# Storing each bf16 part once, reading rows twice, and five copied blocks in place of three

## What is computed

```python
q = (layernorm(x) @ Wq + bq).reshape(B, S, H, DK)      # B 8, S 512, H 16, DK 16
k = (ctx @ Wk + bk).reshape(B, S, H, DK)
v = (ctx @ Wv + bv).reshape(B, S, H, DK)
scores = einsum('bqhd,bkhd->hbqk', q, k) / sqrt(DK)
attn = softmax(scores.reshape(H * B, S, S), axis=0)    # over all heads and batches
x = x + tanh(g_xattn) * (einsum('hbqk,bkhd->bqhd', attn, v) @ Wo + bo)
x = x + tanh(g_ffn) * ffn(layernorm(x))                # int8-like fake quantisation
```

## Time and profile before

| What | Value |
|---|---|
| Median of three runs | 854.2 us (851.15 to 855.73) |
| Profiled execution | 855.71 us, span 853.6 us |
| TensorE, VectorE, ScalarE, GpSimd busy | 740.9, 757.1, 680.9, 474.8 us |
| `prepare` | 0 to 130.2 us, DMA share 0.85 |
| `maxima` | 130.2 to 315 us, DMA share 0.66 |
| `attend`, `ffn` | 315 to 853.6 us |
| Moved by DMA | 165.87 MB |
| Stores of the blocks | 80 of 256 KB |
| Copies in DRAM | 20, of 512 KB or 1,024 KB |

### The profile page before, as it was taken

How to read it: one execution, slowest core, us unless ns; L and a number is a source line. 1 busy time by engine, 2 the same in 40 slices (tenths; PEclk the granted TensorE clock), 3 DMA queues, 4 the chain that set the end, 5 groups by cost and what they waited for, 6 DMA issues and landing times. The chain is left out here.

```text
span 853.6 us, 20038 instructions
## 1 busy us (share of the span) xinstructions
PE 740.9 (87%) x8129; PEld 447.5 (52%) x8151; DVE 757.1 (89%) x825; ACT 680.9 (80%) x1094; POOL 474.8 (56%) x225
## 2 busy tenths in 40 slices
PE   8897897777777769999999999999999999559977
PEld 6564372111212225677666777677777677424334
DVE  4799646999999978999999999999999995758957
ACT  3444448999999979899998999999999834759873
POOL 1233454000000000999999999999999997415500
PEclk9999998999999989999999999999999999879989
DMA  9897798766766627668867787868867794000014
GB/s 294 276 305 225 218 276 208 197 174 172 194 175 174 239 91 235 186 185 281 264 190 206 236 291 212 225 197 288 260 194 213 242 312 138 0 1 1 1 50 147
DMA packets 98442, 165.87 MB, mean 194 GB/s; under 512 B 9712, under 2 KB 37104, under 8 KB 98032
## 3 DMA queue, kind: packets, MB, share of 16 engines
q1 hardware_dynamic: 98352, 164.60, 64.3%
HBM read 134.42 MB, written 42.73 MB: 208 GB/s over the span
## 5 line engine op out<-in xcount | busy, mean ns | idle before, releaser
L1011 POOL TENSOR_TENSOR e<-e,recip 128x1792 f32<-128x1792 f32 (+3 forms) x128 | 367.9, 2919 | 19.3 <-DVE recip L1042 19.2
L963 ACT ACTIVATE e<-psY 128x512 f32<-128x512 f32 x512 | 296.3, 646 | 33.7 <-PE psY L896 28.2
L1029 DVE TENSOR_REDUCE partial<-e 128x128 f32<-128x4096 f32 (+1 forms) x80 | 283.3, 3559 | 7.2 <-ACT e L963 7.2
L896 PE MATMUL psY<-arena 128*128 128x128 bf16 x2048 | 200.6, 221 | 1.8 <-DMA arena<-k_stack 1.7
L896 PEld LDWEIGHTS psY<-arena 128*128 128x128 bf16 x2048 | 149.3, 98 | 75.8 <-issue 26.1
L699 ACT ACTIVATE copies<-ps_max 128x1024 bf16<-128x1024 f32 x189 | 175.9, 1045 | 0.6 <-PE ps_max L678 0.6
L892 PE MATMUL psY<-shift,minus 128*128 128x512 bf16 x396 | 153.1, 387 | 10.9 <-PEq L633 5.5
L715 DVE TENSOR_TENSOR high<-copies,high 128x3072 bf16<-128x3072 bf16 x63 | 109.8, 1744 | 0.0
L1002 POOL MEMSET ones_w<- 96x128 bf16 x1 | 0.2, 206 | 174.0 <-POOLq L633 174.0
L912 PE MATMUL psX<-e,arena 128*32 128x128 f32 x2048 | 76.2, 288 | 3.0 <-issue 1.3
L296 POOL TENSOR_TENSOR parts<-rest,parts 128x512 bf16<-128x512 f32 x32 | 37.5, 1177 | 73.7 <-ACT parts L440 73.6
(11 more groups left out here) (170 smaller groups left out, 1005.8 us busy)
## 6 DMA issues: line engine op xcount, KB each, us to landing
arena<-k_stack SPq DMA_DIRECT2D x256, 256.0 KB, 3.3
arena<-q_stack SPq DMA_DIRECT2D x64, 256.0 KB, 4.4
k_stack<-parts SPq DMA_DIRECT2D x40, 256.0 KB, 3.6
q_stack<-parts SPq DMA_DIRECT2D x40, 256.0 KB, 3.5
arena<-in_x_dram SPq DMA_DIRECT2D x8, 1024.0 KB, 10.8
k_stack<-k_stack SPq DMA_DIRECT2D x12, 512.0 KB, 11.4
arena<-in_ctx_dram SPq DMA_DIRECT2D x4, 1024.0 KB, 6.7
arena<-q_stack SPq DMA_DIRECT2D x8, 512.0 KB, 8.2
```

What stands on the lines that cost most here:

```text
L896: last = nc.tensor.matmul(bank[:, j * P:(j + 1) * P], ks[:, i % KRING, b * P:(b + 1) * P], qs[:, h, b * P:(b + 1) * P], start=False, stop= ...
L963: nc.scalar.activation(e_at(p, half * HB, (half + 1) * HB).rearrange("p q z i -> p z q i"), ps[n % SCORES][:].rearrange("p (z q i) -> p z ...
L1011: nc.gpsimd.tensor_tensor(part, part, by_pairs(recip[:, r % 2, :], share), ALU.mult).then_inc(pool_scaled, 1)
L1029: nc.vector.tensor_reduce(partial[:, :, k, :], e[:, t:t + n].rearrange("p t q z i -> p q i t z"), AX.XY, ALU.add).then_inc(sum_done, 1)
```

## The change

Each part is written once: keys to blocks 0, 1, 2 and queries to blocks 0, 3, 6, three stores for each unit, 48 in all. The arrangement of the finished stacks is another one, with the same eight products: keys 0 1 2 0 1 2 0 1, queries 0 0 0 1 1 1 2 2. The other five blocks of each chunk are copied, in two transfers for the keys (three blocks, then two) and two for the queries (blocks 1, 4, 7, then 2, 5). That is 16 transfers of 1,536 or 1,024 KB, issued 2, 2, 3, 2, 3, 2, 2, 0 behind the loads of the eight couples. Since the maxima use only written blocks, `load_pair` reads key blocks 0 and 1 twice (two transfers of 32 partitions for a key tile) and each of query blocks 0 and 3 twice (four transfers of 16 partitions for a head). A couple has 12 load transfers in place of 4, with the same bytes, and the semaphore counts follow.

```diff
--- before.py
+++ after.py
@@ -37,13 +37,13 @@
 
 
 
-K_PARTS = (0, 0, 1, 1, 2, 2, 0, 1)
-Q_PARTS = (0, 1, 0, 1, 0, 1, 2, 2)
-K_WRITTEN = (0, 1, 2, 3, 4)
-Q_WRITTEN = (0, 1, 2, 3, 6)
+K_WRITTEN = (0, 1, 2)
+Q_WRITTEN = (0, 3, 6)
 WRITES = len(K_WRITTEN)
-K_COPIED = ((5, 4, 1), (6, 0, 1), (7, 2, 1))
-Q_COPIED = ((4, 0, 2), (7, 6, 1))
+K_COPIED = (((3, 6), (0, 3)), ((6, 8), (0, 2)))
+Q_COPIED = (((1, 8, 3), (0, 7, 3)), ((2, 6, 3), (0, 4, 3)))
+K_MAX_ROWS = ((0, 2), (0, 2))
+Q_MAX_ROWS = ((0, 1), (0, 1), (3, 1), (3, 1))
 
 
 def row_copies(is_q, c):
@@ -53,16 +53,16 @@
 
 STACK_COPIES = (row_copies(0, 0) + row_copies(1, 0) + row_copies(0, 1) + row_copies(0, 2) + row_copies(0, 3)
                 + row_copies(1, 1) + row_copies(1, 2) + row_copies(1, 3))
-COPIES_A_COUPLE = 3
+COPIES_OF_COUPLE = (2, 2, 3, 2, 3, 2, 2, 0)
 
 
 def copy_rows(sp, k_stack, q_stack, what, k_copied, q_copied):
 
 
-    is_q, c, dst, src, n = what
+    is_q, c, dst, src = what
     stack, done = (q_stack, q_copied[c]) if is_q else (k_stack, k_copied[c])
-    sp.dma_start(stack[c, :, dst * DK:(dst + n) * DK, :].rearrange("h d x -> h (d x)"),
-                 stack[c, :, src * DK:(src + n) * DK, :].rearrange("h d x -> h (d x)")).then_inc(done, 16)
+    rows = stack[c].rearrange("h (r d) x -> h r (d x)", d=DK)
+    sp.dma_start(rows[:, slice(*dst), :], rows[:, slice(*src), :]).then_inc(done, 16)
 
 
 def bcast_rows(vec, n):
@@ -106,19 +106,27 @@
 EARLY_ITEMS = SCORES + 1
 
 
+EVEN_PIECES = len(K_MAX_ROWS) + 2 * len(Q_MAX_ROWS)
+ODD_PIECES = len(K_MAX_ROWS)
+
+
 def load_pair(sp, p, k_stack, q_stack, even, odd, both, loaded):
 
 
-    def rows(stack, h):
-        return stack[:, h, 0:HALF, :].rearrange("c p x -> p c x")
+    def rows(tile, stack, h, plan):
+        at = 0
+        for first, n in plan:
+            sp.dma_start(tile[at:at + n * DK], stack[:, h, first * DK:(first + n) * DK, :].rearrange("c p x -> p c x")
+                         ).then_inc(loaded, 16)
+            at += n * DK
 
     if even is not None:
-        sp.dma_start(even[0:HALF], rows(k_stack, 2 * p)).then_inc(loaded, 16)
+        rows(even[0:HALF], k_stack, 2 * p, K_MAX_ROWS)
     if both is not None:
         for j in range(2):
-            sp.dma_start(both[j * HALF:(j + 1) * HALF], rows(q_stack, 2 * p + j)).then_inc(loaded, 16)
+            rows(both[j * HALF:(j + 1) * HALF], q_stack, 2 * p + j, Q_MAX_ROWS)
     if odd is not None:
-        sp.dma_start(odd[HALF:P], rows(k_stack, 2 * p + 1)).then_inc(loaded, 16)
+        rows(odd[HALF:P], k_stack, 2 * p + 1, K_MAX_ROWS)
 
 
 def prepare(nc, sem, x, ctx_in, wq, bq, wk, bk, wv, bv, wg, wu, wd, k_stack, q_stack, keep):
@@ -273,11 +281,11 @@
                                       keep["first_loaded"])
                         sp.wait_ge(s["part2_ready"], 2 * (u + 1))
                         sp.wait_ge(s["part3_ready"], 2 * (u + 1))
-                        stack, plan, written = ((k_stack, K_PARTS, K_WRITTEN), (q_stack, Q_PARTS, Q_WRITTEN))[m]
+                        stack, written = ((k_stack, K_WRITTEN), (q_stack, Q_WRITTEN))[m]
                         h0 = dc * (H // DC)
-                        for r in written:
+                        for part, r in enumerate(written):
                             sp.dma_start(stack[c, h0:h0 + H // DC, r * DK:(r + 1) * DK, :].rearrange("h d x -> d h x"),
-                                         parts[:, u % GB, plan[r], :]).then_inc(stacked[u % GB], 16)
+                                         parts[:, u % GB, part, :]).then_inc(stacked[u % GB], 16)
 
                 for i in range(GB):
                     sp.wait_ge(stacked[i], 16 * WRITES * len(range(i, NC * 2 * DC, GB)))
@@ -639,9 +647,9 @@
                     if p:
                         load_pair(sp, p, k_stack, q_stack, k_even[p % 2], None, q_both[p % 2], even_loaded[p % 2])
                     load_pair(sp, p, k_stack, q_stack, None, k_odd[p % 2], None, odd_loaded[p % 2])
-                    if p:
-                        for what in STACK_COPIES[COPIES_A_COUPLE * (p - 1):COPIES_A_COUPLE * p]:
-                            copy_rows(sp, k_stack, q_stack, what, keep["k_copied"], keep["q_copied"])
+                    first = sum(COPIES_OF_COUPLE[:p])
+                    for what in STACK_COPIES[first:first + COPIES_OF_COUPLE[p]]:
+                        copy_rows(sp, k_stack, q_stack, what, keep["k_copied"], keep["q_copied"])
 
                 sp.dma_start(keep["wT_dram"], keep["wT"][:]).then_inc(keep["wT_saved"], 16)
                 sp.wait_ge(keep["wT_saved"], 16)
@@ -660,11 +668,11 @@
                     h, bp = g // GROUPS, g % GROUPS
                     p = h // 2
                     if bp == 0 and h == 0:
-                        pe.wait_ge(keep["first_loaded"], 16 * 3)
+                        pe.wait_ge(keep["first_loaded"], 16 * EVEN_PIECES)
                     elif bp == 0 and h % 2 == 0:
-                        pe.wait_ge(even_loaded[p % 2], 16 * 3 * ((p + 1) // 2))
+                        pe.wait_ge(even_loaded[p % 2], 16 * EVEN_PIECES * ((p + 1) // 2))
                     elif bp == 0:
-                        pe.wait_ge(odd_loaded[p % 2], 16 * (p // 2 + 1))
+                        pe.wait_ge(odd_loaded[p % 2], 16 * ODD_PIECES * (p // 2 + 1))
                     if bp == 0 and 1 <= h <= 3:
                         pe.wait_ge(tiles_zeroed, h)
                     k_head = (k_even, k_odd)[h % 2][p % 2]
```

## The result

The changed kernel takes 848.04 us (median of 20 runs, 843.21 to 853.57), the kernel before 852.30 us (20 runs, 850.46 to 856.34). The ratio is 0.9946, 95% interval 0.9929 to 0.9962: 4.3 to 4.6 us faster, where I had forecast 1.9 us slower. A second series of runs gave 0.9929 (0.9905 to 0.9952).

What follows compares the result with a forecast made beforehand. Bounds: ScalarE and VectorE in the maxima; in the preparation VectorE's pace, then the last store. Sum: 855.7 - 0.5 (preparation) + 2.4 (late loads) = 857.6 us profiled, 856 us from the median; 8-in-10 range 851.5 to 868.

Steps and rivals of the forecast that it cites:

- the price of the stores: Preparation: 48 stores in place of 80, 8 MB fewer, ScalarE's longest wait about gone; gain on the path 1.18 us.
- gain on the path 1.18 us: Preparation: VectorE's 1.18 us loss behind ScalarE's longest store wait goes; 0 if VectorE then finds another wait.
- end of the preparation: minus 0.5 us: Next stage starts at 129.6 against 130.17 us, part of the 1.2 us gain hidden behind slower loads.
- rival C: Preparation gains more: minus 5.3 us for all waits on stores, 1.2 for the last store; 848 us, chance 0.05.
- The last store: End of the preparation: the last store stays what is late next, by 1.8 us over ScalarE's end.
- The load pieces: Loads of the maxima, per 1,024 KB: keys over 32 partitions 4.8 us as before, queries over 16 partitions 10.2 us.
- my own sign of being wrong: Loads of the maxima: the prediction is wrong if small pieces overlap with one another; priced 1.28 us a 16-partition piece.
- The wait in the maxima: Loads late at couples 1, 3, 5, 7 by 0.8, 2.2, 2.4, 0.1 us; the largest stays, plus 2.4 us.
- Copies behind the maxima and SP's issues: `keep_wT` lands near 294 us, attention's loads still in time; 12 load issues a couple, 7.4 us, hidden: no cost.
- A: Loads of the maxima: small pieces cost nothing, queries still at 205 GB/s, nothing late; 852 us, chance 0.25.
- B: DMA queue bounds the maxima: measurably slower from 1.33 us a 16-partition piece, 868 or so at 1.5; chance 0.25.

Runs made afterwards that it cites:

- before_store_first: Kernel before with the last unit's five stores moved ahead of the first load of the maxima, not behind it: 853.23 us, ratio 0.9995.

## Why the prediction was wrong

**The step that failed** is the price of the stores: "gain on the path 1.18 us", and with it "end of the preparation: minus 0.5 us". The runs put it at some 4 us: five stores put back cost 7.0 us in the times and 3.9 us at the start of the maxima, and taking ScalarE's waits away with a fourth slot alone gave 3.6 to 3.8 us in the times. I had counted 5.3 us of ScalarE's waits on stores, left out the third, 2.0 us on q_stack (so rival C's "all waits on stores" is 7.3, not 5.3), and let only the first pass on, since TensorE was busy behind 97 us in the one trace. But TensorE ran at the lower clock from 98 to 102 us of that trace, and this hid the store queue. In the second trace it had the full clock there and started 2.35 us earlier, and the same queue gave 4.50 us of wait to VectorE and 2.1 to TensorE. Two limits of nearly the same length stood in line, and I priced the removal of one as if the other were fixed.

**The last store.** I had the stage end on it at 129.1 us. It landed at 123.1 and 125.3 us: the loads began at 109.4 and 109.7 us, not at 112.6, and the eight query pieces landed within 5.7 and 7.6 us in place of 10.2. That it is late next, by up to 1 us, was right for two of the traces; that it is worth something was not, by `before_store_first`.

**The load pieces.** The key pieces of 32 partitions were priced right: 201 GB/s and more. A piece of 16 partitions takes some 0.95 us at the rate of couple 7, not 1.28, a third more: the overlap of pieces, my own sign of being wrong, is what the two orders point to. A couple then needs 4.8 + 7.6 + 6.3 = 18.7 us of 22.4, or 20.2 with the 9.1 us in which the pieces of couple 7 landed, and the queue catches up, so there is no wait at couples 3 and 5, where I had 2.2 and 2.4 us.

**The wait in the maxima** came, at couple 1 alone: 3.9 and 1.3 us, against 0.8. The mechanism was right, the terms were not. Couple 0 took 21.15 us, not 22.4, so the queries were needed 1.3 us sooner. The last of them landed 24.9 us after the first issue in the first trace and 22.3 in the second, where I had 23.2: by the landings the copies in front took 7.3 us in both, not 6.3, and the eight query pieces 10.3 and 7.4 us, the last two of them late in the first trace.

**Copies behind the maxima and SP's issues** cost nothing, as forecast: `keep_wT`, issued at 268.39 us, was saved before 284.05, when SP issued the loads of attention, 3.1 us earlier than before.

**The rivals.** A had the pieces too fast and the total too slow (852). B didn't come. C, the one with the right sign and size (848), I gave 5%. That its sum meets the result is in part luck: the waits on stores are confirmed, at some 4 us and not at 5.3, and the 1.2 us for the last store are not.

**What stays open.** The 7.0 us between five and three stores in the times, of which a trace shows 3.9; where in the preparation the gain of four slots arises, as its one trace doesn't show it; why VectorE's quantising takes 0.9 us more or less in an instruction; and what the wait at couple 1 is worth.

## What to carry to other kernels

A wait that is partly hidden in one trace is a second limit right behind the first: price its removal with both at their fastest, or read two traces, above all where the granted clock or another engine's pace moves the one limit from execution to execution. To free such a wait, one more buffer slot can do as much as cutting the traffic; here each gave most of the same 4 us, and together not more. Cutting the loads into smaller transfers left their rate as it was down to 32 partitions; at 16 it fell by a third, and where the queue had rest even this didn't change the total by an amount that the runs can tell.

## What the runs showed of the hardware that I had not expected

- The rate of loads with rows of 2 KB went by the partitions of a transfer and not by its size: 128 KB over 64 partitions some 200 to 235 GB/s, 256 KB over 32 partitions 201 to 246, 128 KB over 16 partitions 140 GB/s, and 122 when each second piece went 32 partitions further.
- Four products of 128 x 512 in fp32 took 1.96 us in nine traces and 2.9 to 3.65 us in five at the same place, behind the same 2.35 us of rest, with three and with five stores alike; the mean granted clock in 28 to 36 us is 1.00 in the nine and 0.79 in the five, so for part of it TensorE was at the lower of its two levels, 1.2 GHz.
- The same VectorE instruction on 128x1408 took 1.84 us in one trace of the kernel before and 0.88 in the other. With the place of the lower clock this makes single traces of one kernel differ by some 3 us.
